# A software-pipelined GLA layer on one core: squares, roots, Newton steps and transposes in another order

## The reference, cut to what matters

```python
x = x + gla_block(layernorm(x))      # x: 16 x 256 x 128, this change works here
x = x + graph_ffn(layernorm(x))      # six nodes of 8-head attention, behind it

# gla_block(h): n tokens of 128, 4 heads of 16 (q, k) and 32 (v), chunks of 64
a = rms(h) * w;  q, k, v = a @ Wq, a @ Wk, a @ Wv
b = cumsum(log_sigmoid(a @ Wgk1 @ Wgk2 + bgk2) / 16)         # per chunk
o = tril((q e^b)(k e^-b)^T) v + (q e^b) S,  S = S e^blast + k'^T v
x2 = (rms(o) * gnorm_w * silu(a @ Wg)) @ Wo + h
n = rms(x2) * w;  out = x2 + (silu(n @ W_gate) * (n @ W_up)) @ W_down
```

## Time and profile before

| | |
|---|---|
| median of 3 runs | 1005.67 us (1001.79 to 1007.44) |
| the profiled execution | 1005.67 us, its span 1003.9 us |
| busy, share of the span | PE 95%, DVE 83%, ACT 69%, POOL 45% |
| first stage | to about 256 us |
| mean granted TensorE clock | 0.983 |

### The profile page before, as it was taken

The page is one execution under the profiler, slowest core; times in us unless marked ns, Lnnn a source line. Parts: engine busy times, 40 slices in busy tenths (PEclk is TensorE's granted clock), DMA queues, the critical chain, the costliest instruction groups (busy, mean ns, idle before and its releaser), DMA issues.

```text
span 1003.9 us, 26486 instructions
## 1 busy us (share of the span) xinstructions
PE 956.7 (95%) x9591; PEld 679.4 (68%) x9591; DVE 833.1 (83%) x1879; ACT 692.2 (69%) x1520; POOL 452.7 (45%) x883
## 2 busy tenths in 40 slices
PE   8898888889799999999999999999999999999995
PEld 4665555655577777777777777777777777777763
DVE  4467877865699989989899899989889889989995
ACT  4356556665477777767767778877776777777775
POOL 3623232334343543454453456666444345444455
PEclk9989999999899999999999999999999999999998
DMA  9100000002334433433443434444443343443421
GB/s 244 34 1 1 2 0 0 0 1 84 127 130 143 158 129 135 164 131 129 165 136 130 165 135 140 154 162 141 138 166 131 135 164 131 137 163 130 138 90 33
DMA packets 109528, 112.88 MB, mean 112 GB/s; under 512 B 23355, under 2 KB 83519, under 8 KB 109407
## 3 DMA queue, kind: packets, MB, share of 16 engines
q1 hardware_dynamic: 108478, 111.09, 33.0%
q0 software_dynamic: 128, 0.14, 0.2%
q10 hardware_dynamic: 800, 0.05, 0.1%
HBM read 6.90 MB, written 2.10 MB: 9 GB/s over the span
## 4 chain that ended last, share of the span: by engine, by line
PE 80%; DVE 7%; ACT 5%; issue 2%; POOL 1%; DMA 0%; SPq 0%; DVEq 0%; ACTq 0%; POOLq 0%
PE bank L1336 80%; ACT region L727 1%; DVE region L1194 1%; DVE region L1114 1%; DVE region L1126 1%; ACT region L857 1%; ACT region L746 1%; DVE region L1003 1%; PE bank L1510 1%; ACT region L833 0%; ACT region L741 0%; DVE region L959 0%; DVE region L1121 0%; ACT region L805 0%; DVE region L1042 0%
## 5 line engine op out<-in xcount | busy, mean ns | idle before, releaser
L1194 DVE TENSOR_REDUCE region<-bank 128x2 f32<-128x512 f32 x768 | 494.0, 676 | 67.5 <-PE bank L1336 57.4
L857 ACT ACTIVATE region<-bank 128x512 f32<-128x512 f32 x768 | 406.5, 600 | 175.1 <-PE bank L1336 165.1
L1336 PE MATMUL bank<-st 64*128 64x256 f32 x3072 | 311.1, 326 | 6.5 <-DVE region L1194 5.3
L1336 PEld LDWEIGHTS bank<-st 64*128 64x128 f32 x3072 | 245.4, 192 | 22.0 <-DVE region L1194 7.2
L1336 PE MATMUL bank<-region 128*32 128x256 f32 (+5 forms) x3618 | 232.7, 370 | 4.1 <-POOL region L596 2.0
L1336 PEld LDWEIGHTS bank<-region 128*32 128x32 f32 (+3 forms) x3618 | 123.7, 114 | 81.4 <-issue 7.5
L628 POOL TENSOR_TENSOR mxp<-region,one_col 128x16 bf16<-128x16 f32 x96 | 20.8, 216 | 339.0 <-DVE region L1194 339.0
L1336 PE MATMUL bank<-mst,ones 64*128 64x512 bf16 x768 | 150.9, 387 | 0.5 <-ACT region L857 0.2
L609 POOL TENSOR_TENSOR hl<-qk,hl 128x512 fp32r<-128x512 f32 x96 | 122.5, 1276 | 7.5
L606 POOL TENSOR_TENSOR hl<-qk,one_col 128x512 fp32r<-128x512 f32 x96 | 99.8, 1039 | 10.0 <-ACT qk L822 9.9
L1336 PEld LDWEIGHTS bank<-mst,ones 64*128 64x128 bf16 x768 | 37.3, 93 | 85.0 <-issue 38.6
(11 more groups left out here) (194 smaller groups left out, 1219.4 us busy)
## 6 DMA issues: line engine op xcount, KB each, us to landing
st<-hl SPq DMA_DIRECT2D x384, 256.0 KB, 2.6
mst<-mrows SPq DMA_DIRECT2D x384, 4.0 KB
out<-xall SPq DMA_DIRECT2D x14, 128.0 KB, 2.5
xall<-in_L_attn_hidden_states SPq DMA_DIRECT2D x1, 768.0 KB, 8.5
cst<-in_constants SPq DMA_DIRECT2D x1, 514.5 KB, 4.1
xT<-in_L_ffn_Wq SPq DMA_DIRECT2D x1, 384.0 KB
xT<-in_L_ffn_Wk SPq DMA_DIRECT2D x1, 384.0 KB
xT<-in_L_ffn_Wv SPq DMA_DIRECT2D x1, 384.0 KB
```

The lines of the kernel that those rows point to most:

```text
L857: act.activation(to, x_bank(x, k, e)[:, :].rearrange("p (j q) -> p j q", j=2), ACT.Exp).then_inc(B["exp_ok"], 1)
L1194: dve.tensor_reduce(mx[s.n % 2][:, to:to + 2], s_bank(s, k, e)[:, :].rearrange("p (j k) -> p j k", j=2), AX_X, ALU.max, negate=True).then_ ...
L1336: return pe.matmul(o, w, x, start=start, stop=stop, skip_group_check=skip)
```

## The change

It moves groups of instructions within a slot, on four places of three engines, and changes no instruction. On ACT, the squares of `x2` go ahead of the `keT` copies, the root of `ve2` ahead of that of `ve`, the root of `ve3` behind the square and copy of `o`. On DVE, `bn_stats` goes ahead of the Newton steps of `ve3`; `x1_rows` goes from behind `qke` to ahead of `uu`; the scaling and Newton steps of `ve2` go ahead of scores 0 and 1; silu 0 and 1 go ahead of the Newton steps of `ve` and the rows `hh`. On PE, the transposes of `n` go from behind up 1 to ahead of the scores of tiles 2 and 3.

```diff
--- before.py
+++ after.py
@@ -734,6 +734,13 @@
                     gate_tanh(j, 1)
                     if k is None:
                         phase(*stages(2))
+                if k is not None:
+                    act.wait_ge(A["x2_ok"].sem, A["x2_ok"].at(k))
+                    for t in range(TPI):
+                        n = act.activation(nn[:, t, :], x2[:, t, :], ACT.Square, accum_out=ss[:, t:t + 1])
+                    n.then_inc(A["ss_ok"].sem, 1)
+                    if draining:
+                        act.preload_act_table_set(LOGS)
                 if i is not None:
                     act.wait_ge(A["keT_ps"], i + 1)
                     for odd in range(2):
@@ -741,16 +748,9 @@
                         n = act.activation(keT[r, :, odd * QK:odd * QK + QK], quads(2)[r, :, QK:2 * QK], ACT.Copy)
                     n.then_inc(A["keT_ok"], 1)
                 if k is not None:
-                    act.wait_ge(A["x2_ok"].sem, A["x2_ok"].at(k))
-                    for t in range(TPI):
-                        n = act.activation(nn[:, t, :], x2[:, t, :], ACT.Square, accum_out=ss[:, t:t + 1])
-                    n.then_inc(A["ss_ok"].sem, 1)
-                    if draining:
-                        act.preload_act_table_set(LOGS)
+                    inverse_root(ve2, rr2, k, "ve2_ok", "r2l", "r2a")
                 if f is not None:
                     inverse_root(ve, rr, f, "ve_ok", "rl", "ra")
-                if k is not None:
-                    inverse_root(ve2, rr2, k, "ve2_ok", "r2l", "r2a")
                 if j is not None and not draining:
                     gate_tanh(j, 0)
                     gate_tanh(j, 1)
@@ -783,12 +783,12 @@
                     act.activation(za, za, ACT.Exp).then_inc(A["e_ok"].sem, 1)
                     act.wait_ge(A["e_ok"].sem, A["e_ok"].at(f))
                     act.activation(za, za, ACT.Ln, bias=1.0).then_inc(A["l_ok"].sem, 1)
-                if j is not None:
-                    inverse_root(ve3, rr3, j, "ve3_ok", "r3l", "r3a")
                 if i is not None:
                     act.wait_ge(A["o_ps"].sem, A["o_ps"].at(i))
                     act.activation(sq, bank[0][:, :], ACT.Square).then_inc(A["sq_ok"].sem, 1)
                     act.activation(osb, bank[0][:, :], ACT.Copy).then_inc(A["o_ok"].sem, 1)
+                if j is not None:
+                    inverse_root(ve3, rr3, j, "ve3_ok", "r3l", "r3a")
                 if i is not None:
                     if isinstance(i, int) and i == 0:
                         act.wait_ge(S["we_t"], 1)
@@ -937,8 +937,6 @@
 
             def first(f, i, k, j):
                 e = late(j)
-                if e is not None:
-                    newton(dve, ve3, rr3, rt3, e, "r3a", "r3b", "r3c", "rstd3_ok")
                 if f is not None:
                     if i is None:
                         dve.wait_ge(L["x_first"], 16)
@@ -949,6 +947,10 @@
                     for t in range(TPI):
                         n = dve.bn_stats(bst[:, t, :], xall[:, ds(TPI * f + t, 1), :])
                     n.then_inc(A["bn1"].sem, 1)
+                if e is not None:
+                    newton(dve, ve3, rr3, rt3, e, "r3a", "r3b", "r3c", "rstd3_ok")
+                    dve.wait_ge(A["rstd3_ok"].sem, A["rstd3_ok"].at(e))
+                    x1_rows(e)
                 if k is not None:
                     dve.wait_ge(A["t1_ok"], k + 1)
                     dve.wait_ge(A["rstd_ok"].sem, A["rstd_ok"].at(k))
@@ -957,9 +959,6 @@
                     dve.wait_ge(A["eb_ok"], i + 1)
                     dve.wait_ge(A["qkp_ps"], i + 1)
                     dve.tensor_tensor(qke, bank[2][:, :], eb, ALU.mult).then_inc(A["qke_ok"], 1)
-                if e is not None:
-                    dve.wait_ge(A["rstd3_ok"].sem, A["rstd3_ok"].at(e))
-                    x1_rows(e)
                 if f is not None:
                     dve.wait_ge(A["bn1"].sem, A["bn1"].at(f))
                 if k is not None:
@@ -984,12 +983,16 @@
                     times_up(j, 1)
                     if k is None:
                         maxes(stages(3)[2], 1)
+                if k is not None:
+                    dve.wait_ge(A["ss_ok"].sem, A["ss_ok"].at(k))
+                    dve.tensor_scalar(ve2, ss, 1.0 / D, RMS_EPS, ALU.mult, ALU.add).then_inc(A["ve2_ok"].sem, 1)
+                    newton(dve, ve2, rr2, rt2, k, "r2a", "r2b", "r2c", "rstd2_ok")
                 if i is not None:
                     scores(i, 0)
                     scores(i, 1)
-                if k is not None:
-                    dve.wait_ge(A["ss_ok"].sem, A["ss_ok"].at(k))
-                    dve.tensor_scalar(ve2, ss, 1.0 / D, RMS_EPS, ALU.mult, ALU.add).then_inc(A["ve2_ok"].sem, 1)
+                if j is not None and not draining:
+                    silu_gate(j, 0)
+                    silu_gate(j, 1)
                 if f is not None:
                     newton(dve, ve, rr, rt, f, "ra", "rb", "rc", "rstd1_ok")
                     dve.wait_ge(A["rstd1_ok"].sem, A["rstd1_ok"].at(f))
@@ -1005,11 +1008,6 @@
                     n.then_inc(A["h_ok"], 1)
                     if i is None:
                         scale_first()
-                if k is not None:
-                    newton(dve, ve2, rr2, rt2, k, "r2a", "r2b", "r2c", "rstd2_ok")
-                if j is not None and not draining:
-                    silu_gate(j, 0)
-                    silu_gate(j, 1)
                 if isinstance(i, int) and i == 0:
                     dve.wait_ge(L["wo_in"], 16)
                     dve.tensor_scalar(wo[:, :], wo[:, :], cols[:, 2:3], 0.5, ALU.mult, ALU.mult)
@@ -1398,6 +1396,8 @@
                         warm(4)
                 if e is not None:
                     transpose_x1(e, 2)
+                if k is not None and f is not None or i is not None and k is not None:
+                    transpose_n(k)
                 if i is not None:
                     for t in range(2, TPI):
                         pe.wait_ge(A["am_ok"], TPI * i + t - 1)
@@ -1412,9 +1412,6 @@
                         up(j, m)
                     if last:
                         scores(stages(3)[2], 1)
-                if k is not None and i is not None:
-                    transpose_n(k)
-                if j is not None:
                     pe.wait_ge(A["hid_ok"], j * MT + 1)
                     gate(j, 2)
                     pe.wait_ge(A["hid_ok"], j * MT + 2)
```

## The result

The changed kernel takes 1010.4 us, median of 19 runs (1005.51 to 1013.53), against 1005.68 us for the kernel before (19 runs, 1000.0 to 1007.74): ratio 1.0052, 95% interval 1.0033 to 1.0072. I had forecast 1004.9 us in a range up to 1009.0. All ratios are against runs of the kernel before taken together with the runs in question, and leave out runs more than 1.5% above the fastest of their kernel. The profiled execution took 1007.08 us around a span of 1005.3. Busy times and the number of matmuls are those of before; PE's mean clock is 0.986 against 0.983.

What follows compares the result with a forecast made beforehand. The prediction took a chain through four engines, with no engine always busy, to bound each slot (one start of L805 to the next). Its slot terms summed to -0.8 us from 1005.67 us: 1004.9 us, range 1000.8 to 1009.0.

Steps and rivals of the forecast that it cites:

- Slot 1: Slot ahead of the loop: earlier `n` helps PE, POOL's last state product comes 1.5 us later; -0.3 us in all.
- PE gains 0.4: In slot 1, PE was to gain 0.4 us, with `n` 3 us earlier but `hh` held until 61.1.
- Loop slots at full clock: Sign of being right: loop slots of about 25.7 us at a granted clock of 1.00.
- The rival that the clock falls there all the same: Rival, chance 0.20: smaller PE gaps still bring half clock, +1.06 us a slot in three slots, 1008.1 us.
- A slot of 25.68: Loop slot at full clock: silu 2 0.96 us earlier than in slot 5, `qke` 0.19 later; slots 4 to 6 together -1.2.
- Newton of `ve3` held by POOL: End of the slot: first Newton step waits for POOL's L575, ending at 181.18; 0.19 us on the chain through `qke`.
- `hh` between silu 1 and times_up 0 as the new limit: Middle of the slot, DVE: times_up 0 starts at 167.75, not 166.47, and gate 2 waits for it.
- Slot 3: First pass of the hardware loop: rows now ahead, `qke` 3.46 us after `eb`; 28.2 us against 28.32, -0.1.
- Slot 2: Slot before the hardware loop, without rows, which kept its clock before: +0.5 us.
- Slots 7 and 8: Slots behind the loop: slot 7 -0.2 us from earlier transposes, slot 8 +0.5 us from a delayed `uu`.
- The sum: All slot terms added: -0.8 us, giving 1004.9 us; the sum as worked had a chance of 0.46.

Runs made afterwards that it cites:

- after_fill: The changed kernel with idle matmuls in three PE gaps: ahead of the products with `keT`, the transposes of `n` and gate 2; 1008.02 us, ratio 1.0044.
- after_slot1: The changed kernel with six idle matmuls in slot 1 alone, ahead of PE's wait for the last state product; 1007.24 us, ratio 1.0020.
- undo_silu: The changed kernel with silu 0 and 1 put back behind the Newton steps of f and the rows `hh`; 1017.13 us, ratio 1.0137.
- undo_k: The changed kernel with squares back behind `keT`, DVE's work for k behind scores 0 and 1, transposes behind up 1; 1010.72 us, ratio 1.0047.
- undo_rows: The changed kernel with `x1_rows`, the Newton steps and the root of `ve3` put back in their old places; 1007.25 us, ratio 1.0030.
- before_fill: The kernel before with seven idle matmuls in PE's gap ahead of up 0, slots 2 to 7; 1000.69 us, ratio 0.9966.
- mid_fill: The kernel before with seven idle matmuls ahead of up 0, and gate 2 ahead of the transposes of `n`; 998.26 us, ratio 0.9936.
- rows_fill: The kernel before with seven idle matmuls ahead of up 0, plus only the change's `x1_rows`, Newton steps and root of `ve3`; 1004.34 us, ratio 1.0005.
- mid_fill2: The kernel before with seven idle matmuls, gate 2 ahead of the transposes of `n`, and silu 2 ahead of three state products; 1015.31 us, ratio 1.0106.
- silu_pool: The changed kernel with silu 0 and 1 back behind `hh`, and POOL's sum L588 moved behind its state products; 1008.33 us, ratio 1.0054.

## Why the prediction was wrong

Slot 1 is the step that failed. The prediction had "PE gains 0.4" there, and the later state product coming 1.5 later, "just ahead of PE's use at 67.85: -0.3". POOL's product is nearly right (1.7 later within the slot). But PE gained 1.5 and not 0.4, because its idle matmuls and the transposes ahead of them no longer ran at half clock, which I hadn't counted. So it waits 1.43 us where I had no wait. That the slot's time came out near the forecast in the first profile (34.48 us against 34.57 before, -0.1 where I had -0.3) is in part luck: POOL sets the moment at which the products start, and not PE. And I put no price on the gap itself. The clock fell behind it in the second profile, where slot 1 is 4.6 us longer. Of the 36 runs listed with their clocks 19 take 1010 us or more; with the gap filled none of 12 does, and the median is 3.2 us lower. I had asked of the loop slots alone what a gap does to the clock. Of the 5.5 us by which the forecast is off, these are 3.2. Nearly all the rest, 2.2, stands in the profile that has no such stretch (1007.1 against 1004.9), and its terms follow.

Point by point, the rest:

- *Loop slots at full clock.* Right for slots 4 to 6 in all four profiles (the two of the changed kernel, after_fill, after_slot1), and for slot 3 in the two of the changed kernel. The rival that the clock falls there all the same was wrong in its place; the clock fell in slots 1 and 2. But it was not far off: slot 3 lost 2.1 us in after_fill, behind the gap of 1.8 us at the loop's entry, which the prediction hadn't listed.
- *A slot of 25.68.* 26.02. The terms off: `qke` 0.33 late and not 0.19, as the rows start 0.16 behind the last Newton step, a gap I hadn't counted; and tanh 2 1.14 behind the start of gate 2 and not 0.89. Most of that is a reading of mine. In the chain of slot 6 before, the piece of gate 2 starts at 194.39, where the transposes end; its first matmul starts at 194.23, so that from start to start it was 1.05 us to tanh 2, and 0.16 of the 0.25 was never there to gain. Of the other 0.09 the cause stays open. Idle matmuls ahead of gate 2 (after_fill) left the slot at 26.02. 3 x 0.34 is 1.0 us.
- *Newton of `ve3` held by POOL.* Right: 1.00 us, and the 0.31 us confirmed from both sides. The Trainium skill ("SBUF — State Buffer", "Who interferes with whom") has a DVE instruction with two SBUF inputs and a GpSimd one that reads SBUF exclude each other; L1077 here (1.00 us, to 0.01 behind the end of L575), and L1077 in undo_silu (1.22 us, and 0.14 when L588 was moved), agree.
- *`hh` between silu 1 and times_up 0 as the new limit.* Right; times_up 0 starts 12.13 behind `eb` (forecast 12.07). That the early work of k and the silus are one price, paid once, I had not seen; undo_silu and undo_k show it.
- *Slot 3.* -0.1 forecast, +0.3 came (28.65 against 28.32), and +2.0 at equal clock: 1.3 by the rows (undo_rows), the rest the 0.74 of each slot. *Slot 2:* +0.5 forecast, +0.8 at full clock and +1.45 in the first profile, with a stretch at half clock. *Slots 7 and 8:* +0.3 forecast; from the `eb` that ends slot 6 to the end of the span the two kernels take 796.6 and 796.7 us, +0.1.
- *The comparison.* The sum set three slots of before at half clock in part against slots at full clock. For the profiled execution of before that was fair, and the profiled one of the changed kernel came to 1007.1 and not 1004.9: 1.0 of it lies in slots 4 to 6, 0.9 in slot 2, 0.4 in slot 3, and the rest cancels. A second profile of a kernel whose three runs span 0.56% would have been needed to say which of its slots lose the clock how often; I took one execution for the rule.

## What to carry to other kernels

Compare two orders at one clock first: a profile whose slots of the same work differ in length has both levels in it, and the runs' clocks beside their times show the rest, roughly (before_fill at a mean of 0.986 takes 1002.3 to 1003.6 us, the kernel before 1001.5 to 1002.6, though none of slots 1 to 6 is longer in its profile). When an engine's work is moved ahead, list every new gap on TensorE, in the written-out slots and at the entry of the loop as well, and look at the granted clock behind it in more than one profile. A wait of DVE for a short answer of ACT is cheap only while DVE has nothing that will stand on the chain later; and a small two-input DVE instruction should not be due while POOL is in a long one.

## What the runs showed of the hardware

- A gap of 1.43 us between dense matmuls was followed by 10.2 us at 1.2 GHz in one execution and by none in another of the same kernel (39.06 and 34.48 us for the slot). PE had no idle time in the 10.2 us; matmuls on one column stood in them, and whether that matters no run tests. With six idle matmuls in the gap, none of 12 runs took more than 1008.1 us (1005.5 to 1013.5 without).
- Seven idle bf16 matmuls in a gap of 1.95 us came with 2.4 GHz in all loop slots of before_fill and mid_fill, where before three of four had lost 1.7 us; in rows_fill one loop slot still fell (slot 3, 0.94) and in mid_fill2 two (slots 3 and 5, 0.89 and 0.88).
- The same wait of 1.81 to 1.84 us at the loop's entry was followed by 2.4 GHz in the two profiles of the changed kernel and by 1.2 GHz in after_fill, where the slot took 30.74 us instead of 28.65.
- A DVE instruction on 8 elements a row took 1.22 us instead of 0.14 while POOL added 512 columns of SBUF (undo_silu, silu_pool), and one on 4 elements 1.00 instead of 0.16.
